# Storing a group's values three slots sooner, and moving reloads and gathers in the fill of a paged-attention residual kernel

## The reference

```python
x = x + _L0_cond_ref(x, itok_B_1_198, L0_cond_weights)      # a 32x32 matrix per sequence, picked by index
x = x + _L1_cond_ref(x, Wq, Wk, Wv, Wo, ..., block_tables, kv_lens)   # paged attention
x = x + _L2_cond_ref(x, itok_B_0_7, L2_cond_weights)         # again a picked 32x32 matrix
x = x + _L3_cond_ref(x, W, A, Bm, scalings, adapter_idx)     # dense weight plus a picked rank-16 adapter
```

```python
k_blocks = k_blocks.at[blk, :, off, :].set(k.transpose(0, 2, 1, 3))
v_blocks = v_blocks.at[blk, :, off, :].set(v.transpose(0, 2, 1, 3))
k_all, v_all = k_blocks[block_tables], v_blocks[block_tables]      # reshaped by head
allowed = (kpos <= pos) & (kpos > pos - WINDOW)
p = softmax(where(allowed, einsum(q, k_all) * SCALE, -inf));  o = einsum(p, v_all) @ Wo
```

## Time and profile before

| | us |
|---|---|
| median of 3 runs | 533.43 |
| lowest, highest | 529.5, 533.53 |
| the profiled execution | 534.09 |
| its span | 531.7 |
| granted TensorE clock, mean | 0.92 |
| PE, DVE, ACT, POOL busy | 416.2, 339.5, 319.5, 160.2 |

### The profile page before, as it was taken

The page is one execution under the profiler, slowest core; times in us unless marked ns, Lnnn a source line. Parts: engine busy times, 40 slices in busy tenths (PEclk is TensorE's granted clock), DMA queues, the critical chain, the costliest instruction groups (busy, mean ns, idle before and its releaser), DMA issues.

```text
span 531.7 us, 15926 instructions
## 1 busy us (share of the span) xinstructions
PE 416.2 (78%) x5302; PEld 338.6 (64%) x5302; DVE 339.5 (64%) x1156; ACT 319.5 (60%) x1018; POOL 160.2 (30%) x180
## 2 busy tenths in 40 slices
PE   2566897967753439985997987999799899899996
PEld 1355786855531327774776776777677777677774
DVE  7865699624136127782787776777588788787541
ACT  3357674648431526754776686676676777766761
POOL 5200555460041302531323333243233333312000
PEclk9998998889775557997999999999899999999999
DMA  7998775394375746775686786867768769657400
GB/s 191 387 299 312 204 242 183 130 239 119 118 158 134 144 116 149 150 207 104 166 176 144 193 182 175 178 135 184 158 161 217 155 162 241 154 159 147 72 22 22
DMA packets 87755, 90.25 MB, mean 170 GB/s; under 512 B 22459, under 2 KB 83675, under 8 KB 84992
## 3 DMA queue, kind: packets, MB, share of 16 engines
q1 hardware_dynamic: 69744, 49.57, 38.5%
q0 software_dynamic: 9600, 32.21, 23.2%
q10 hardware_dynamic: 8376, 8.03, 4.6%
HBM read 79.20 MB, written 35.39 MB: 216 GB/s over the span
## 4 chain that ended last, share of the span: by engine, by line
DMA 33%; PE 31%; DVE 11%; SPq 8%; issue 8%; ACT 7%; ACTq 1%; DVEq 0%
DMA values_by_group<-new 23%; PE bank L1460 6%; DMA q_spill<-end_room 5%; SPq L1078 3%; PE bank L1496 3%; PE bank L1449 3%; PE score_banks L1399 3%; PE bank L1430 3%; DMA xin<-in_x_dram 3%; PE bank L1364 2%; DMA blocks_room<-q_spill 2%; PE score_banks L1478 2%; PE score_banks L1350 2%; ACT pT_room L1251 2%; PE bank L1450 1%
## 5 line engine op out<-in xcount | busy, mean ns | idle before, releaser
L1242 ACT ACTIVATE p_room<-score_banks,nmax 128x176 f32<-128x176 f32 x256 | 100.9, 400 | 69.8 <-DVE nmax L791 56.2
L917 POOL TENSOR_TENSOR rms<-rms,halfpow 128x8 f32<-128x8 f32 x30 | 54.7, 1824 | 188.1 <-DVE rms L598 188.0
L1460 PE MATMUL bank<-ident,p_room 128*88 128x128 f32 x512 | 84.2, 288 | 27.5 <-ACT pT_room L1251 20.4
L1251 ACT ACTIVATE pT_room<-bank 88x512 f32<-88x512 f32 x128 | 75.5, 590 | 18.1 <-PE bank L1460 17.2
L791 DVE TENSOR_REDUCE nmax<-score_banks 128x2 f32<-128x352 f32 x128 | 61.0, 518 | 38.8 <-PE score_banks L1478 38.4
L1460 PEld LDWEIGHTS bank<-ident,p_room 128*88 128x88 f32 x512 | 53.3, 127 | 45.1 <-issue 23.3
L1279 ACT ACTIVATE new<-old 88x512 f32<-88x512 f32 x56 | 34.8, 626 | 34.0 <-DMA values_by_group<-new 33.7
L1242 ACT ACTIVATION_READ_ACCUMULATOR p_room<-score_banks,nmax 128x1 f32 x256 | 50.8, 198 | 0.0
L1496 PE MATMUL bank<-pT_room,blocks_room 88*32 88x64 f32 x1024 | 23.9, 234 | 25.3 <-ACT norm L1261 22.7
L1496 PEld LDWEIGHTS bank<-pT_room,blocks_room 88*32 88x32 f32 x1024 | 18.0, 117 | 35.1 <-ACT pT_room L1251 24.1
L783 DVE COPY blocks_room<-bank 128x352 f32<-128x352 f32 x64 | 33.0, 515 | 10.7 <-PE bank L1425 10.5
(11 more groups left out here) (247 smaller groups left out, 923.0 us busy)
## 6 DMA issues: line engine op xcount, KB each, us to landing
values_by_group<-new SPq DMA_DIRECT2D x16, 704.0 KB
blocks_room<-values_by_group SPq DMA_DIRECT2D x64, 88.0 KB
v_room<-values_by_group SPq DMA_DIRECT2D x64, 88.0 KB
xin<-in_x_dram SPq DMA_DIRECT2D x32, 128.0 KB
x_spill<-v_room SPq DMA_DIRECT2D x32, 128.0 KB
written_blocks<-new ACTq DMA_DIRECT2D x2, 2048.0 KB, 6.9
xin<-x_spill SPq DMA_DIRECT2D x32, 128.0 KB
out_dram<-end_room SPq DMA_DIRECT2D x32, 128.0 KB
```

The lines of the kernel that those rows point to most:

```text
L917: pool.tensor_tensor(out=rms[:, i, 2, :], in0=rms[:, i, 1, :], in1=halfpow[:, :], op=ALU.pow).then_inc(s_rstd, 1)
L1242: last = a.activation(pex[:, k // 2 % 2, g, :], ps_u[half][:, i, 0:KEYS], ACT.Exp, bias=nmax[:, k // 2 % 2, g:g + 1], accum_out=rsum[:, k ...
L1251: a.activation(pT[:, 2 * half:2 * half + 2, :, :].rearrange("p g c r -> p (g c r)"), ps_t[0:HK, :], ACT.Copy).then_inc(s_ptc, 1)
L1460: last = turn_over(ps_t[0:HK, at:at + 128], pex[:, (k // 2 - 1) % 2, 2 * half + i, HK * c:HK * c + HK], ident[:, :])
```

## The change

Four things move; nothing is added to or taken from what is computed, and each DMA is issued as often as before.

1. In the loop, the store of a group's values moves from slot 0 of its block to slot 5 of the block ahead. Its wait for the gather of `new` (semaphore `new_in`) goes with it.
2. On SP the four reloads of x and the two of queries move from behind all spills to behind the 23rd spill. The store of group 0 follows the 30th spill, its load follows that, then the store of group 1, and only then the wait for all spills.
3. On ACT and DVE the refill of `new0` in block 0 moves from slots 0 and 1 to slots 2 and 3.
4. On POOL the `old` gather of group 3 moves into slot 0 and waits for the store of group 0; the `new` gather of group 2 moves from slot 0 to slot 4.

```diff
--- before.py
+++ after.py
@@ -358,8 +358,8 @@
 
         def pieces_in_slot(k, by_slot):
 
-            if k in (0, 1):
-                return 0, (2 * k, 2 * k + 1)
+            if k in (2, 3):
+                return 0, (2 * (k - 2), 2 * (k - 2) + 1)
             kk = k + EARLY
             if k < 4 or kk // 8 + 2 >= NG:
                 return 0, ()
@@ -974,19 +974,25 @@
                 pool.wait_ge(s_order[i], 8)
                 past_waits()
                 fetch_new(i, rd_idx[0:ROWS, 1, i:i + 1])
-            for i in range(2):
-                fetch_old(i, rd_idx[0:ROWS, 0, i + 2:i + 3])
+            fetch_old(0, rd_idx[0:ROWS, 0, 2:3])
 
 
             def slot(it, k):
                 b = 16 * it + k
                 for n in rope_tiles(k, 0):
                     rstd(rope_of_tile(4 * it + n), n % 2)
-
-
+                if k == 0:
+                    pool.wait_ge(s_vst[0], 16)
+                    past_waits()
+                    fetch_old(1, rd_idx[0:ROWS, 0, 3:4])
+
+
+                if k == 4:
+                    pool.wait_ge(s_gnew[0], 16)
+                    gather_new(0, 2, 16)
                 kk = k + EARLY
                 i, j, grp = (kk // 8) % 2, kk % 8, kk // 8 + 2
-                if j == 4 and k >= 0 and grp < NG:
+                if j == 4 and k > 0 and grp < NG:
                     fills = it + kk // 16 + 1
                     pool.wait_ge(s_gnew[i], 16 * fills)
                     gather_new(i, 2 * it + grp, 8 * fills + 8)
@@ -1040,19 +1046,36 @@
                     sp.wait_ge(s_dset, mark["w1"])
                     sp.dma_start(w2_d, wpick[1][:, :]).then_inc(s_pickw[1], 16)
 
+            def store_values(i, g):
+                sp.dma_start(v_d[g, :, :].rearrange("(r o) c -> r o c", o=BLOCK), new[i][0:ROWS, :, 1, :]).then_inc(s_vst[i], 16)
+
+            def load_values(i, g):
+                by_key = v_d[g, :, :].rearrange("(f w o c) d -> o w f (c d)", f=GB, w=W, c=2)
+                for o in range(HB):
+                    sp.dma_start(vg[i][W * o:W * o + W, :, :, :].rearrange("p f c d -> p f (c d)"), by_key[o]).then_inc(s_vin[i], 16)
+
             for u in range(2):
                 sp.sem_inc(s_out[u], 16)
             for i, n in enumerate(QUERIES):
                 if n >= 2:
                     sp.wait_ge(s_qc, i + 1)
                     sp.dma_start(q_d[n, :, :], q1_tile(n)).then_inc(s_qsp[spilled.index(n) % 4], 16)
+                if n == 28:
+                    for u in range(4):
+                        sp.wait_ge(s_spill[u], 16 * (NT // 4))
+                        sp.dma_start(xin[u][:, :], x1_d[u, :, :]).then_inc(s_x1[u], 16)
+                    for m in (2, 3):
+                        at = spilled.index(m)
+                        sp.wait_ge(s_qsp[at % 4], 16 * (at // 4) + 16)
+                        sp.dma_start(qs[m - 2][:, :], q_d[m, :, :]).then_inc(s_q[m - 2], 16)
+            sp.wait_ge(s_gnew[0], 16)
+            store_values(0, 0)
+            sp.wait_ge(s_vst[0], 16)
+            load_values(0, 0)
+            sp.wait_ge(s_gnew[1], 16)
+            store_values(1, 1)
             for u in range(4):
                 sp.wait_ge(s_qsp[u], 16 * len(spilled[u::4]))
-                sp.wait_ge(s_spill[u], 16 * (NT // 4))
-            for i in range(2):
-                sp.dma_start(qs[i][:, :], q_d[i + 2, :, :]).then_inc(s_q[i], 16)
-            for u in range(4):
-                sp.dma_start(xin[u][:, :], x1_d[u, :, :]).then_inc(s_x1[u], 16)
 
             def slot(it, k):
                 grp = k // 8 + 1
@@ -1061,21 +1084,13 @@
                         sp.wait_ge(s_rope, ROPE * rope_of_tile(4 * it + n) + ROPE)
                         past_waits()
                         sp.dma_start(qs[n % 2][:, :], q_d[4 * it + n + 2, :, :]).then_inc(s_q[n % 2], 16)
-                if grp < NG:
-                    i, fills = grp % 2, it + grp // 2
-                    if k % 8 == 0:
-                        sp.wait_ge(s_gnew[i], 16 * fills + 16)
+                if k % 8 == 3 and k > 0 and grp < NG:
+                    sp.wait_ge(s_vst[grp % 2], 16 * (it + grp // 2) + 16)
+                    if grp >= 2:
                         past_waits()
-                        sp.dma_start(v_d[2 * it + grp, :, :].rearrange("(r o) c -> r o c", o=BLOCK), new[i][0:ROWS, :, 1, :]).then_inc(s_vst[i], 16)
-                    if k % 8 == 3:
-                        sp.wait_ge(s_vst[i], 16 * fills + 16)
-                        if grp >= 2:
-                            past_waits()
-                            sp.wait_ge(s_pv, 8 * it + GB // 2 * (grp - 1))
-                        past_waits()
-                        by_key = v_d[2 * it + grp, :, :].rearrange("(f w o c) d -> o w f (c d)", f=GB, w=W, c=2)
-                        for o in range(HB):
-                            sp.dma_start(vg[i][W * o:W * o + W, :, :, :].rearrange("p f c d -> p f (c d)"), by_key[o]).then_inc(s_vin[i], 16)
+                        sp.wait_ge(s_pv, 8 * it + GB // 2 * (grp - 1))
+                    past_waits()
+                    load_values(grp % 2, 2 * it + grp)
                 for kind, n in fin_step(k):
                     if kind == "x2" and n + 4 < NT:
                         await_copied(sp, (kind, n), it)
@@ -1083,6 +1098,11 @@
                     if kind == "x4":
                         await_copied(sp, (kind, n), it)
                         sp.dma_start(out_t[4 * it + n, :, :], x4s[n % 2][:, :]).then_inc(s_out[n % 2], 16)
+                if k % 8 == 5 and k > 0 and k // 8 + 2 < NG:
+                    grp = k // 8 + 2
+                    sp.wait_ge(s_gnew[grp % 2], 16 * (it + grp // 2) + 16)
+                    past_waits()
+                    store_values(grp % 2, 2 * it + grp)
 
             run_slots(sp, slot)
             for u in range(2):
```

## The result

| | before | after |
|---|---|---|
| median | 532.79 (4 runs) | 502.24 (4 runs, 494.17 to 508.18) |
| the profiled execution | 534.09 | 508.18 |
| span | 531.7 | 506.4 |

A forecast was written before the change was run, and what follows sets the result against it. Bound: ACT's refill waiting for stores of the values, 33.7 us, with PE waiting behind it. 534.1 less 10 (fill) less 14 (loop) gave 510 us, a gain of 24; range 498 to 523.

The forecast's parts named there:

- the loop term: Loop: nearly all store waits go, 14 us gained, between 12 from bare waits and 17.0; bounds 4 and 23 us.
- 40.4 us: Loop: best round of before, with one store wait of 0.4 us; six such rounds would make the loop 242.4 us.
- Rival B: Deeper gain: best round itself held up by late loads; loop gains 23 us, fill 14, total 497; chance 0.15.
- The mechanism: Loop: store issued seven slots, 17.7 us, ahead of ACT's refill, lands in 11.2 to 18.2 us, so nearly all waits go.
- The fill, 10 us: Fill: stores 0 and 1 issued and landed sooner, so ACT's second store wait ends 10 us sooner; bounds 0 and 16.
- The second wait: Fill: ACT's refill in slot 4 waiting for store 1, 8.9 us before, stays at some 6 us.
- My lower bound of 0: Fill: no gain if both stores take 18.2 us and the reloads cost 3.7.
- the other 3.7: Fill: upper bound of the reloads' cost, added to 152 and 18.2 for store 0's latest landing, 174 us.
- Rival A: Slow store: every loop store takes about 18 us; loop gains 6, fill 8, total 520 us; chance 0.20.
- always of the slow kind: Loop: by queue order, the store behind eight loads and beside POOL's old gather is always slow; loop gain 4, total 520.
- Rival C: Slower: loop stores past the 17.7 us distance; break-even at 20 us, 547 us total at 21; chance 0.06.
- Rival D: Nothing: slot 5's store waits for a late gather, only a smaller fill gain comes; 531 us; chance 0.07.

The follow-up runs named there:

- the repetition: The changed kernel run again unaltered, six executions: 501.92 us, ratio to before 0.952.
- e5: Kernel before, with stores of groups 1 to 15 cut to an eighth and all loads reading group 0's values: 510.23 us, ratio 0.963.
- e2: Kernel before with only the loop's edit, the store in slot 5 for groups 2 to 15: 514.58 us, ratio 0.975.
- e10: Changed kernel with the six reloads behind store 0 instead of behind spill 23: 503.17 us, ratio 0.949.
- e8: Changed kernel with group 1's store issued ahead of the eight loads of group 0 in the fill: 504.94 us.
- e4: Changed kernel with the eight value loads moved from slot 3 to slot 6, behind the store of slot 5: 534.6 us, ratio 1.014.
- e6: Changed kernel with stores of groups 1 to 15 cut to an eighth and all loads reading group 0's values: 495.8 us, ratio 0.932.
- e9: Changed kernel with group 3's old gather put back right behind group 2's, without its wait for store 0: 503.6 us, ratio 0.949.

## Why the prediction came out as it did

**The step that failed is the size of the loop term, "I take 14 us".** The loop gave 16.8 us in the profiled execution and 22 in the repetition, close to my bound of 23. Two things in the term were too small. First, six rounds of 40.4 us gave 17.0, and I took 3 us off "because part of a round's excess has other causes". e5 has no store wait in its loop and rounds of 40.3 us on average, and its loop is 18 us shorter than that of before: nearly the whole excess belonged to the stores, their waits, clock and traffic together. Second, "40.4 us", the best round of before, was no floor. Rounds without a store wait take 38.7 to 39.5 us in after and 38.6 to 39.4 in e2. The trace of before has no two blocks in a row under 40.1, so no row of it could give them. Rival B had this size for the loop, but its reason, that "the best round was itself held up by late loads", is not borne out: e5 takes 40.4 us in rounds without a store wait. Why the changed loop mostly runs the shorter rounds stays open. B's half of the fill (14 us) did not come.

**Part of the distance is likely chance.** Fill and loop give 25.7 us in one pair of traces and 31 with the repetition's. The first ratio, 35 us, has no trace behind it, and the repetition's ratio, 26 us, is near my 24.

**The mechanism was right.** ACT's refill waits once in the fill (7.1 us, forecast 3 to 9) and for 3.8 us in the rest (forecast under 2; none in the repetition). A store is issued seven slots ahead and seldom late. The loop's clock rose with it, from 0.97 to 0.99. Slot 3's loads were issued 7.5 to 9.6 us after the start of the block in eight of the twelve blocks (forecast 7 to 9), and 10.2 to 14.4 us after it in four.

**The fill, 10 us: measured 8.9.** Store 0 went at 150.4 (forecast 152) and took 12.5 us (12.5). Store 1 went at 166.0 (168) and took 20.3 (17), landing at 186.3 (185). I took the eight loads ahead of it as the main reason for those 17 us, and e10, with the same loads ahead and 8.2 us, speaks against that. The second wait stayed with 7.1 us (6). The first was gone. The reloads cost nothing seen: ACT waits 7.7 us for spills, 7.2 before at the same instruction. My lower bound of 0 counted the reloads' time twice, in the 152 and again in "the other 3.7"; by its own terms it is 1.4 us.

**Where small steps failed.** SP still waits 35.1 us for stores (23.7 + 11.4), 21.4 in the repetition; forecast was under 20. The 11.4 us from store 0 to its loads stood in the 48.6 before too, as some 7 us, and I had not counted them among what stays. In the fill a new line did stand partly for the old one: PE's 7.9 us for the values of group 0. Store 0 landed 10.9 us sooner, but the products that need it began 7.1 us sooner (175.65 against 182.71 us); e8 makes this wait 9.7 us while it takes ACT's away.

**Rival A, the slow store,** was right on duration at places (18.7 and 20.3 us) and wrong on the time. The Trainium skill, page "DMA: Bandwidth & Descriptors", section "Queues, rings and completion order", has a DMA engine take one queue's descriptors in ring order. e4 agrees: with the order of loads and store swapped the lateness swaps too, though its loads are also issued later. But "always of the slow kind" does not follow from it: the store stands behind the loads in every block, and in nine of the twelve in after it had landed when the next loads were issued, 10.4 to 15.7 us after it; in the repetition SP waited for it once in the twelve, for 0.3 us. **Rival C** would need stores of 20 us or more each time in the loop; the longest measured there took 18.7, and one in the fill 20.2. **Rival D** fell with the first trace.

A single execution of after lies anywhere in 494 to 508 us and one of before in 521 to 538. The medians and ratios carry the statements above; fill and loop figures of one trace carry them only where a second trace agrees.

## What to carry to other kernels

When a buffer wait is taken away by issuing a DMA sooner, compare the slots between issue and need with the slowest durations in the trace, not the median: five slots helped little, seven did nearly all. On a queue with a large store and loads, put the one with slack second, and look at what other queues issue at that moment before the order on one queue is blamed for a slow DMA. Do not take the best round of a stalled kernel as the floor of the loop; work it out with a kernel whose suspected cost is removed, and look at all of its rounds, since they differ.

## What the runs showed of the hardware

- Rounds of the same instructions, at a granted clock of 1.00 and without a store wait, took 38.6 to 39.4 us in e2, 39.3 to 40.5 in e5, 39.3 to 40.7 in e6 and 40.2 to 40.7 in e8. In e5 and e6 the length changed by over 1 us within one execution.
- A store of 704 KB directly behind eight loads of 88 KB on its queue took 20.2 us with a gather issued 2.2 us ahead of it (after), and 8.2 us with the gather issued 2.0 us behind it (e10).
- The issue of a small query load took SP 12.82 us directly behind a store of 1408 pieces (10.98 in the repetition, 10.71 before), but 2.98 in e9 and 3.74 in e10 at the same place, and 0.36 us at the median of the 28 such loads of after. In e10 four reloads took 9.73 us behind store 0, where they take 1.87 ahead of it. SP issued nothing else meanwhile.
- In the block of after with ACT's wait of 2.6 us PE stood idle for 3.0 us up to 312.7 us. The clock was 1.00 in that pause and up to 314 us, 0.53 in the 2 us from there, 0.61 in the next 2 and 1.00 again from 318, so for some 4 us it was largely at the lower of its two levels, 1.2 GHz:

```profile
310.00:312.00 2.00, 0.00 (x0) 0.00 (x0) 1.04 (x4) 1.35 (x3) 0.00 (x0) 1.00 0.61 141
312.00:314.00 2.00, 1.30 (x38) 1.22 (x39) 0.52 (x2) 1.32 (x6) 0.00 (x0) 1.00 0.68 92
314.00:316.00 2.00, 2.00 (x7) 1.42 (x6) 1.93 (x7) 1.88 (x6) 1.01 (x1) 0.53 0.50 109
316.00:318.00 2.00, 2.00 (x9) 1.76 (x8) 0.64 (x2) 1.34 (x3) 0.98 (x2) 0.61 0.78 157
318.00:320.00 2.00, 2.00 (x56) 1.39 (x54) 0.56 (x2) 0.54 (x2) 0.87 (x1) 1.00 0.81 147
```

The block took 22.6 us, against 19.1 for the block of this place in a round at 1.00: 0.9 us of it are not ACT's wait.
